# Attention on one Trainium2 chip: reciprocal of the softmax sums read from PSUM, and AV matmuls three chunks behind QK

## The chip, the cores and the metric

The kernel runs on all 8 cores of one Trainium2 chip. Each core computes two of the 16 sequences, with no exchange between cores. The time is device microseconds of the slowest core.

## What is computed

The input x has 16 sequences of 2048 tokens and 1024 features, all float32. One layer with attention (16 heads of 64) and a feed-forward part with a router follows, each with a layer norm in front and one behind:

```python
q = (x @ Wq + bq)                      # 16 heads of 64
k = ((x @ Wk + bk) @ Wl + bl)
v = ((x @ Wv + bv) @ Wl + bl)
attn = jax.nn.softmax(jnp.einsum('bhqd,bhkd->bhqk', q, k) * scale, axis=-1)
out = jnp.einsum('bhqk,bhkd->bhqd', attn, v)
attn_out = out @ Wo + bo
...
x = x + _layernorm(attn_out_of(_layernorm(x)))
x = x + _layernorm(ffn_of(_layernorm(x)))
```

The change lies in the softmax and the product with v alone.

## The kernel before

The program runs five phases with a barrier between them: A0 (norm and projections of the first sequence), B0 (its attention), A1, B1, and C (residual, norms and feed-forward of both sequences). There is no scheduler. Every phase appends small functions to a list for each engine (Q["T"] for PE, Q["V"] for DVE, Q["S"] for ACT, Q["Y"] for the DMA queue of SP), and these lists are each engine's order. inc() raises the engine's semaphore after the last thing appended, and waits are written out by hand. On DVE and ACT, inc() adds a drain (L166), and a wait for it shows in the profile as DVEq L166 or ACTq L166.

Phase B (emit_phase_B, L392) goes over 4 slices of 512 queries (tqc) and in each over 8 pairs of heads (j): 32 pairs in a sequence, 64 in all. For a pair it goes over 16 chunks of 128 keys (tkc):

- emit_qk (L458) multiplies the chunk's keys with the queries of both heads (L467, L471) into one of two PSUM tiles, ps1 or psT (both show as ps or psT, by turns). It waits for the exponential of two chunks before, which frees that tile.
- ACT takes the exponential of the 128x1024 scores (L484) into one of four slots. Two slots are the tile pt_sb, and two lie in xn_tok. It waits for the AV matmuls of four chunks before.
- emit_av (L490) multiplies the exponentials with v for both heads (L499, L502) and adds up over the chunks in av2, 65 rows: 64 of output, and in row 64 the sum of the exponentials, since v has a column of ones. It waits for its exponential, and AV of chunk 0 also for the previous pair's normalisation (attn_done, L493), which reads av2.

The order of the two on PE is set by AVLAG: at step tkc, emit_av(tkc - AVLAG) is appended first and emit_qk(tkc) after it.

After the 16 chunks fden (L519) makes the reciprocals of both heads' sums: 1024 values on one partition. It copies row 64 of av2 (PSUM) to den_sb (SBUF, a part of xn_fm), drains and takes the reciprocal into rden. fdr (L527) spreads them over the partitions by four matmuls with a row of ones (L529, L531), and fnorm (L536) copies these to SBUF (L542) and multiplies (L544, L546) into u_s. In PE's list fdr stands behind the last AV and before the next pair's first QK.

When a slice's 8 pairs are done, its output projection (emit_wo, L413, matmuls L422) is appended to PE in 8 parts among the chunks of the next slice's first pair (j == 0). The last slice of a sequence has it on its own.

Of the kernel before, what the change touches and what calls it, by code (L numbers as in the profile page):

```python
# [31 lines left out]
def build_nc():  # L32
# [33 lines left out]
    with ExitStack() as ctx:  # L66
# [66 lines left out]
        den_sb = fmh[0:1, 0:1024]  # L133
        rden = fmh[0:1, 1024:2048]
# [257 lines left out]
        def emit_phase_B(seq):  # L392
            psTf = psT.bitcast(F32).reshape([128, 1024])
            stb = [ps1[:, 0:1024], psTf[:, 0:1024]]
            av2 = ps2[:, 0:1024]
# [56 lines left out]
            for tqc in range(4):  # L452
                qb = tqc * SLT
                for j in range(8):
# [35 lines left out]
                    def emit_av(tkc):  # L490
                        pp = tkc % 4
                        ed = exp_done[(j, tkc)]
                        wat = attn_done.get(j - 1 if j >= 1 else 7)  # L493
                        def fav(t, j=j, tkc=tkc, pp=pp, ed=ed,
                                avA=avA, avB=avB, wat=wat):
                            t.wait_ge(sS.h, ed)
                            if tkc == 0 and wat is not None:
                                t.wait_ge(sV.h, wat)
                            t.matmul(avA[0:65, :], vt_sb[:, tkc, j, 0:65],  # L499
                                     pslot(pp, 0),  # L500
                                     start=(tkc == 0), stop=(tkc == 15))
                            return t.matmul(avB[0:65, :], vt_sb[:, tkc, j, 65:130],  # L502
                                            pslot(pp, 1),
                                            start=(tkc == 0), stop=(tkc == 15))
                        Q["T"].append(fav)
                        av_done[(j, tkc)] = inc("T", sT)

                    AVLAG = 2
                    for tkc in range(16 + AVLAG):
                        if tkc >= AVLAG:  # L510
                            emit_av(tkc - AVLAG)
                        if tkc < 16:
# [5 lines left out]

                    def fden(v, av2=av2, ad=av_done[(j, 15)]):  # L519
                        v.wait_ge(sT.h, ad)  # L520
                        v.tensor_copy(den_sb[0:1, :], av2[64:65, :])  # L521
                        v.drain()
                        return v.reciprocal(rden[0:1, :], den_sb[0:1, :])  # L523
                    Q["V"].append(fden)
                    den_done = inc("V", sV)
                    drp = drb[par]
# [468 lines left out]
        for ph in phase_list:  # L995
# [21 lines left out]
            elif ph[0] == "B":  # L1017
                seq = int(ph[1])
                load_w("wo", wo_sb)
                barrier()  # L1020
                emit_phase_B(seq)
                barrier()
                if KDBG and seq == 0:
                    qO.n += 16
                    Q["Y"].append(lambda y: y.dma_start(out=ddbg_a, in_=u_s[:]
                                                        ).then_inc(qO.h, 16))
                    qO.n += 16
                    Q["Y"].append(lambda y: y.dma_start(out=ddbg_z0, in_=dzs[0]
                                                        ).then_inc(qO.h, 16))
                    barrier()  # L1030
# [112 lines left out]
```

## Time and profile before

| | us |
|---|---|
| median of 2 runs | 4354.77 (4320.6 and 4388.95) |
| the profiled execution | 4305.65 |
| its span on the slowest core, core 7 | 4304.1 |
| spans of all cores | 4286.0 to 4304.1 |
| PE busy | 2291.9 (53%) |
| DVE busy | 1551.6 (36%) |
| ACT busy | 1310.7 (30%) |

The profile is of one execution. Its span runs from the first to the last instruction of a core. Busy is time in instructions of an engine, PE being TensorE, DVE VectorE and ACT ScalarE. Idle time of an engine is put down to what released it. The granted clock (PEclk) is TensorE's, as a share of full speed: 1.00 is 2.4 GHz and 0.50 is 1.2 GHz.

### The profile page before, as it was taken

How to read it: one execution, taken by the hardware profiler on the slowest of the kernel's cores; microseconds unless marked ns; L12 is line 12 of the kernel's file. 1: busy time of each engine (PE TensorE's matmuls, PEld its weight loads, DVE VectorE, ACT ScalarE, POOL GpSimd, SP SyncE). 2: the span in 40 equal slices, each digit the busy share in tenths (PEclk: the TensorE clock that was granted, in tenths of full speed). 3: DMA queues.
4: the chain of work that ended last, by engine and by line, in shares of the span. 5: the costliest groups of instructions: out<-in, count | busy, mean ns of one | idle time of the engine just before them, and what ended most of it. 6: DMA issues, size and time to landing. Idle time of an engine off the chain costs nothing.

```text
span 4304.1 us, 33363 instructions; the slowest of 8 cores (4286.0 to 4304.1 us)
## 1 busy us (share of the span) xinstructions
PE 2291.9 (53%) x9296; PEld 781.1 (18%) x9296; DVE 1551.6 (36%) x2164; ACT 1310.7 (30%) x1117; POOL 10.1 (0%) x16
## 2 busy tenths in 40 slices
PE   3777555656556554777655655656553333223333
PEld 1333111111111111333211111111111112111121
DVE  2444222323223223444222322323223454455545
ACT  0000355555555550000255555555551000000000
POOL 0000000000000000000000000000000000000000
PEclk9888877777777776888877777777776666566666
DMA  6000100000000003000100000000003212222121
GB/s 119 20 20 1 20 1 0 20 0 0 20 0 20 1 0 78 20 20 1 20 0 0 20 0 1 20 0 20 0 0 88 93 54 83 98 98 98 71 86 59
DMA packets 52842, 137.04 MB, mean 32 GB/s; under 512 B 7479, under 2 KB 7614, under 8 KB 52670
## 3 DMA queue, kind: packets, MB, share of 16 engines
q1 hardware_dynamic: 42206, 117.59, 7.6%
q0 software_dynamic: 10464, 17.32, 2.6%
q8 instruction: 88, 1.44, 0.1%
q14 instruction: 84, 0.69, 0.1%
HBM read 101.87 MB, written 50.33 MB: 35 GB/s over the span
## 4 chain that ended last, share of the span: by engine, by line
PE 36%; DVE 27%; ACT 21%; issue 7%; DMA 5%; DVEq 2%; ACTq 1%; SPq 0%; another core or an unknown queue 0%; POOL 0%; POOLq 0%
PE ps L324 14%; ACT xn_tok L484 10%; DVE xn_fm L523 10%; ACT pt_sb L484 9%; PE ps L499 3%; PE ps L422 3%; PE ps L878 3%; PE ps L529 3%; PE ps L502 2%; DVE xn_fm L521 2%; DMA xst<-z_scr 2%; DVEq L166 2%; PE ps L467 2%; PE psT L467 1%; DVE xn_tok L542 1%
## 5 line engine op out<-in xcount | busy, mean ns | idle before, releaser
L521 DVE COPY xn_fm<-ps 1x1024 f32<-1x1024 f32 x64 | 78.0, 1219 | 1361.3 <-PE ps L502 1361.3
L484 ACT ACTIVATE pt_sb<-ps,cst_sb 128x1024 bf16<-128x1024 f32 x256 | 308.9, 1207 | 779.6 <-PE ps L471 748.1
L523 DVE RECIPROCAL xn_fm<-xn_fm 1x1024 f32<-1x1024 f32 x64 | 418.6, 6541 | 5.1
L529 PE MATMUL ps<-xn_fm,ones_sb 1*64 1x512 f32 x128 | 123.8, 1068 | 520.5 <-DVEq L166 520.5
L324 PE MATMUL ps<-xn_fm,arena 128*128 128x512 bf16 x1536 | 356.0, 395 | 26.3 <-DMA blrow_bf<-blrow 15.5
L499 PE MATMUL ps<-pt_sb,vt_sb 128*65 128x512 bf16 x512 | 223.3, 436 | 262.1 <-ACTq L166 176.2
L484 ACT ACTIVATE xn_tok<-ps,cst_sb 128x1024 bf16<-128x1024 f32 x256 | 308.9, 1207 | 123.8 <-PE ps L471 86.9
L484 ACT ACTIVATE xn_tok<-psT,cst_sb 128x1024 bf16<-128x1024 f32 x256 | 308.8, 1206 | 61.0 <-issue 42.0
L484 ACT ACTIVATE pt_sb<-psT,cst_sb 128x1024 bf16<-128x1024 f32 x256 | 308.8, 1206 | 59.7 <-issue 54.8
L499 PE MATMUL ps<-xn_tok,vt_sb 128*65 128x512 bf16 x512 | 212.6, 415 | 203.3 <-ACTq L166 202.5
L467 PE MATMUL ps<-q_sb,k_sb 64*128 64x512 bf16 x512 | 232.2, 453 | 36.5 <-DMA arena<-wo 36.5
L471 PE MATMUL ps<-q_sb,k_sb 64*128 64x512 bf16 x512 | 232.4, 454 | 0.0
L471 PE MATMUL psT<-q_sb,k_sb 64*128 64x512 bf16 x512 | 229.2, 448 | 0.0
L467 PE MATMUL psT<-q_sb,k_sb 64*128 64x512 bf16 x512 | 229.0, 447 | 0.0
L502 PE MATMUL ps<-pt_sb,vt_sb 128*65 128x512 bf16 x512 | 223.8, 437 | 0.0
L502 PE MATMUL ps<-xn_tok,vt_sb 128*65 128x512 bf16 x512 | 210.7, 412 | 0.0
L277 ACT ACTIVATE sti<-stv 128x4 f32<-128x4 f32 x8 | 1.7, 207 | 646.3 <-DVEq L166 646.3
L596 PE MATMUL ps<-identf_sb,xst 128*128 128x128 f32 x256 | 48.5, 362 | 276.4 <-DMA xst<-z_scr 230.6
L324 PEld LDWEIGHTS ps<-xn_fm,arena 128*128 128x128 bf16 x1536 | 153.4, 101 | 225.0 <-issue 61.3
L735 PE MATMUL psT<-identb_sb,u_s 128*128 128x128 bf16 x256 | 32.4, 305 | 263.9 <-DVEq L166 263.9
L346 DVE TENSOR_SCALAR u_s<-ps,bcols_sb 128x512 bf16<-128x512 f32 x128 | 96.1, 751 | 174.3 <-PE ps L324 174.3
L298 PE MATMUL psT<-identb_sb,xn_tok 128*128 128x128 bf16 x256 | 32.4, 306 | 226.0 <-DVEq L166 226.0
(142 smaller groups left out, 2685.7 us busy)
## 6 DMA issues: line engine op xcount, KB each, us to landing
xst<-x SPq DMA_DIRECT2D x32, 512.0 KB, 7.0
z_scr<-xst SPq DMA_DIRECT2D x64, 256.0 KB, 3.4
xst<-z_scr SPq DMA_DIRECT2D x64, 256.0 KB, 5.3
k_sb<-x SPq DMA_DIRECT2D x32, 512.0 KB, 7.8
x_scr<-q_sb SPq DMA_DIRECT2D x32, 512.0 KB, 2.6
k_sb<-x_scr SPq DMA_DIRECT2D x32, 512.0 KB, 5.1
out<-q_sb SPq DMA_DIRECT2D x32, 512.0 KB, 2.8
arena<-wq POOLq DMA_DIRECT2D x2, 2048.0 KB, 23.1
```

What stands on the lines that cost most here:

```text
L324: r = t.matmul(pa, lhs_get(ki), rhs_get(ki), start=(ki == 0), stop=(ki == n_k - 1 and rider is None))
L346: return v.tensor_scalar(dst_fn(mo), pa, bcols[:, bias0 + mo:bias0 + mo + 1], None, ALU.add)
L422: r = t.matmul(pa, wo_sb[:, ki, mo * 128:(mo + 1) * 128], u_s[:, ki, :], start=(ki == 0), stop=(ki == 7))
L467: t.matmul(stb[pk][:, 0:512], k_sb[0:64, j, tkc * 128:(tkc + 1) * 128], q_sb[0:64, j, qb:qb + SLT], start=True, stop=True, tile_position=( ...
L471: return t.matmul(stb[pk][:, 512:1024], k_sb[64:128, j, tkc * 128:(tkc + 1) * 128], q_sb[64:128, j, qb:qb + SLT], start=True, stop=True, t ...
L484: return sc.activation(pwide(pp), stb[pk][:, 0:1024], AF.Exp, bias=cst[:, 1:2], scale=cst[:, 0:1])
L499: t.matmul(avA[0:65, :], vt_sb[:, tkc, j, 0:65], pslot(pp, 0), start=(tkc == 0), stop=(tkc == 15))
L502: return t.matmul(avB[0:65, :], vt_sb[:, tkc, j, 65:130], pslot(pp, 1), start=(tkc == 0), stop=(tkc == 15))
L521: v.tensor_copy(den_sb[0:1, :], av2[64:65, :])
L523: return v.reciprocal(rden[0:1, :], den_sb[0:1, :])
L529: t.matmul(drp[0:64, :], ones_r[0:1, 0:64], rden[0:1, 0:512], start=True, stop=True, tile_position=(0, 0))
L878: t.matmul(pa, bw_sb[:, ki, mo * 128:(mo + 1) * 128], xn_fm[:, ki, :], start=(ki == 0), stop=False)
```

## The change

Two things are changed, both in phase B. AVLAG goes from 2 to 3, so that each AV is appended one chunk later. And fden no longer copies the sums to SBUF: the reciprocal reads row 64 of av2 in PSUM itself. The copy and the drain behind it are gone. The exponentials' slots, the PSUM tiles and all waits are as before. The lines behind the change stand two lines higher in the changed kernel (L529 is L527 there).

```diff
-                    AVLAG = 2
+                    AVLAG = 3
                     for tkc in range(16 + AVLAG):
                         if tkc >= AVLAG:
                             emit_av(tkc - AVLAG)
...
                     def fden(v, av2=av2, ad=av_done[(j, 15)]):
                         v.wait_ge(sT.h, ad)
-                        v.tensor_copy(den_sb[0:1, :], av2[64:65, :])
-                        v.drain()
-                        return v.reciprocal(rden[0:1, :], den_sb[0:1, :])
+                        return v.reciprocal(rden[0:1, :], av2[64:65, :])
```

PE at the start of the second pair of the first sequence, before. L467 and L471 are QK (into ps1 for even chunks, psT for odd ones), and L499 and L502 are AV:

```order
L467 MATMUL ps1<-q_sb,k_sb 128x512
L471 MATMUL ps1<-q_sb,k_sb 128x512
L467 MATMUL psT<-q_sb,k_sb 128x512
L471 MATMUL psT<-q_sb,k_sb 128x512
L499 MATMUL ps2<-pt_sb,vt_sb 65x512
L502 MATMUL ps2<-pt_sb,vt_sb 65x512
L467 MATMUL ps1<-q_sb,k_sb 128x512
L471 MATMUL ps1<-q_sb,k_sb 128x512
```

The same place in the changed kernel:

```order
L467 MATMUL ps1<-q_sb,k_sb 128x512
L471 MATMUL ps1<-q_sb,k_sb 128x512
L467 MATMUL psT<-q_sb,k_sb 128x512
L471 MATMUL psT<-q_sb,k_sb 128x512
L467 MATMUL ps1<-q_sb,k_sb 128x512
L471 MATMUL ps1<-q_sb,k_sb 128x512
L499 MATMUL ps2<-pt_sb,vt_sb 65x512
L502 MATMUL ps2<-pt_sb,vt_sb 65x512
```

QK of chunk 2 now stands ahead of AV of chunk 0. From there on AV and QK alternate as before, and the pair ends with three AVs in a row instead of two.

PE at the start of a pair that carries the output projection (the first pair of the second slice), before. L422 is one part of the projection, 8 matmuls:

```order
L471 MATMUL psT<-q_sb,k_sb 128x512
L422 MATMUL ps2<-u_s,arena1 128x512 x8
L499 MATMUL ps2<-pt_sb,vt_sb 65x512
L502 MATMUL ps2<-pt_sb,vt_sb 65x512
L467 MATMUL ps1<-q_sb,k_sb 128x512
L471 MATMUL ps1<-q_sb,k_sb 128x512
```

And in the changed kernel:

```order
L471 MATMUL psT<-q_sb,k_sb 128x512
L422 MATMUL ps2<-u_s,arena1 128x512 x8
L467 MATMUL ps1<-q_sb,k_sb 128x512
L471 MATMUL ps1<-q_sb,k_sb 128x512
L499 MATMUL ps2<-pt_sb,vt_sb 65x512
L502 MATMUL ps2<-pt_sb,vt_sb 65x512
```

The projection's part keeps its place behind QK of chunk 1, and QK of chunk 2 and AV of chunk 0 change places behind it.

DVE in one pair, before:

```order
L521 COPY xn_fm<-ps 1x1024
L523 RECIPROCAL xn_fm<-xn_fm 1x1024
L542 COPY xn_tok<-ps 128x512
L544 SCALAR_TENSOR_TENSOR u_s<-ps,xn_tok 64x512
L546 SCALAR_TENSOR_TENSOR u_s<-ps,xn_tok 64x512
```

And in the changed kernel:

```order
L521 RECIPROCAL xn_fm<-ps 1x1024
L540 COPY xn_tok<-ps 128x512
L542 SCALAR_TENSOR_TENSOR u_s<-ps,xn_tok 64x512
L544 SCALAR_TENSOR_TENSOR u_s<-ps,xn_tok 64x512
```

One instruction fewer in each pair, and the source of the reciprocal is now ps.

## Rows read from the trace of the kernel before

**Rows 1.** Windows of phases B0 and B1: us, busy by engine (instructions), PEclk, DMA share, GB/s

```profile
480.00:1636.00 1156.00, 652.94 (x2389) 157.77 (x2390) 333.48 (x186) 619.02 (x513) 0.00 (x0) 0.77 0.02 6
2110.00:3256.00 1146.00, 645.87 (x2373) 155.89 (x2374) 332.17 (x184) 619.03 (x513) 0.00 (x0) 0.78 0.02 6
```

**Rows 2.** Timeline of PE and DVE from one pair to the next: start, duration, [idle before]

```profile
1005.63 0.38 PE L502 MATMUL ps<-xn_tok,vt_sb 128*65 128x512 bf16 x1
1006.11 1.22 DVE L521 COPY xn_fm<-ps 1x1024 f32<-1x1024 f32 x1 [23.00 <-PE ps L502]
1007.41 6.54 DVE L523 RECIPROCAL xn_fm<-xn_fm 1x1024 f32<-1x1024 f32 x1
1014.12 1.08 PE L529 MATMUL ps<-xn_fm,ones_sb 1*64 1x512 f32 x1 [8.12 <-DVEq L166]
...
1016.02 0.60 PE L467 MATMUL ps<-q_sb,k_sb 64*128 64x512 bf16 x1
...
1017.73 0.68 DVE L546 SCALAR_TENSOR_TENSOR u_s<-ps,xn_tok 64x512 bf16<-64x512 f32 x1
...
1018.59 0.60 PE L499 MATMUL ps<-pt_sb,vt_sb 128*65 128x512 bf16 x1 [1.53 <-DVEq L166]
...
1019.56 0.60 PE L467 MATMUL ps<-q_sb,k_sb 64*128 64x512 bf16 x1
...
1021.09 0.60 PE L467 MATMUL psT<-q_sb,k_sb 64*128 64x512 bf16 x1
...
1022.66 0.60 PE L467 MATMUL ps<-q_sb,k_sb 64*128 64x512 bf16 x1
```

**Rows 3.** Timeline of ACT at the same place, exponentials 0 to 4

```profile
1016.79 1.21 ACT L484 ACTIVATE pt_sb<-ps,cst_sb 128x1024 bf16<-128x1024 f32 x1 [11.54 <-PE ps L471]
1018.21 1.21 ACT L484 ACTIVATE pt_sb<-psT,cst_sb 128x1024 bf16<-128x1024 f32 x1 [0.21 <-issue]
1020.32 1.21 ACT L484 ACTIVATE xn_tok<-ps,cst_sb 128x1024 bf16<-128x1024 f32 x1 [0.91 <-PE ps L471]
1021.86 1.21 ACT L484 ACTIVATE xn_tok<-psT,cst_sb 128x1024 bf16<-128x1024 f32 x1 [0.33 <-PE psT L471]
1023.43 1.21 ACT L484 ACTIVATE pt_sb<-ps,cst_sb 128x1024 bf16<-128x1024 f32 x1 [0.37 <-PE ps L471]
```

**Rows 4.** Groups of DVE instructions by line and shape: busy, mean ns, idle before

```profile
L523 DVE RECIPROCAL xn_fm<-xn_fm 1x1024 f32<-1x1024 f32 x64 | 418.6, 6541 | 5.1
...
L521 DVE COPY xn_fm<-ps 1x1024 f32<-1x1024 f32 x64 | 78.0, 1219 | 1361.3 <-PE ps L502 1361.3
...
L252 DVE TENSOR_SCALAR_CACHE_REDUCE pt_sb<-xst 128x1024 f32<-128x1024 f32 x32 | 39.0, 1220 | 46.4 <-DMA xst<-x 39.3 <-issue 7.0
...
L287 DVE TENSOR_SCALAR xn_tok<-xst,stm,sti 128x1024 bf16<-128x1024 f32 x32 | 26.0, 813 | 13.3 <-ACTq L166 6.7 <-issue 6.6
...
L272 DVE RECIPROCAL stv<-stv 128x4 f32<-128x4 f32 x8 | 1.4, 178 | 0.6
```

**Rows 5.** Waits of PE over the span: us in total, times, longest

```profile
PE ps L499 <- DVEq L166: 85.4, 56, 1.5
```

**Rows 6.** Windows (columns as rows 1): in a reciprocal; from a pair's first exponential on

```profile
1010.50:1014.00 3.50, 0.00 (x0) 0.00 (x0) 3.45 (x1) 0.00 (x0) 0.00 (x0) 0.50 0.00 0
1093.66:1101.80 8.14, 6.61 (x19) 1.33 (x18) 1.53 (x3) 6.03 (x5) 0.00 (x0) 0.50 0.00 0
```

**Rows 7.** Waits of ACT over seven pairs of the first sequence, 1093.2 to 1339.5

```profile
ACT pt_sb L484 <- PE ps L471: 83.1, 12, 12.0
...
ACT xn_tok L484 <- PE ps L471: 6.4, 7, 0.9
ACT xn_tok L484 <- PE psT L471: 2.3, 7, 0.3
ACT pt_sb L484 <- PE psT L471: 0.6, 2, 0.3
```

**Rows 8.** Waits of ACT over seven pairs of the second sequence, 2430 to 2677.1

```profile
ACT xn_tok L484 <- PE ps L471: 5.5, 7, 0.9
```

**Rows 9.** Window (columns as rows 1) in a pair that carries the output projection

```profile
1058.00:1082.00 24.00, 24.00 (x113) 8.79 (x112) 5.08 (x7) 16.89 (x14) 0.00 (x0) 1.00 0.00 1
```

## The prediction
> **What bounds the kernel now.** I read the windows by stage first: the two attention stages take 1156 and 1146 us of the 4304.1 us span, and in neither is any engine busy for much over half of it (PE 653, ACT 619, DVE 333 us in the first) [rows 1]. The change touches only them. So the question is which wait ends last in each stretch of one head pair, of which there are 64 (2 sequences, 4 query slices, 8 pairs).
>
> The timeline of one pair's boundary answers it [rows 2]. The last AV matmul (L502) starts at 1005.63, DVE copies the denominators (L521, 1.22 us), computes 1024 reciprocals on one partition (L523, 6.54 us), PE spreads them by matmul (L529, from 1014.12), and only behind that, in PE's order, stand the next pair's QK matmuls (1016.02). ACT sits idle 11.54 us before its first exponential [rows 3]. Everything in that boundary is serial: no other engine works beside it, so a microsecond saved there is a microsecond of the program. Inside a pair, once it runs, the exponentials follow each other with gaps of 0.21 us, one in 1.42 us (1016.79, 1018.21 in [rows 3]): ACT is the bound there and PE waits for it. Between the two lies a short start-up in which ACT waits for PE again: idle 0.91, 0.33 and 0.37 us before exponentials 2, 3 and 4 [rows 3].
>
> **The copy taken out (64 times).** From the start of the copy to the start of the reciprocal is 1007.41 - 1006.11 = 1.30 us [rows 2], copy, drain and issue together. The reciprocal now starts where the copy did, behind the same wait. 64 x 1.30 = 83.2 us, all of it on the path. What I can't read is whether the reciprocal takes 6.54 us when its source is PSUM: no row has that. Two bounds: a copy of 1024 f32 from PSUM takes 1219 ns and a one-element-per-cycle pass over 1024 f32 from SBUF (L252) takes 1220, so the source costs nothing; against that L287, 1024 f32 from SBUF, takes 813, so a source in PSUM could cost up to 0.41 us [rows 4]. Below nothing is excluded, since nothing there makes reading PSUM the quicker. The reciprocal spends (6541 - 178) / 1020 = 6.24 ns on an element (L523 against L272, 4 elements) where the copy spends 1219 / 1024 = 1.19, so its own arithmetic and not its reading should set its pace [rows 4]. I take 0; the other end takes 64 x 0.41 = 26 us back.
>
> The Trainium skill prices this ("VectorE: DVE Perf Modes", the section on the TRN2 errata): a PSUM source has 62 cycles more of fixed cost than one in SBUF, some 65 ns, which by it would be an estimated 4 us less gain in all. The pair L521 and L252 shows no such difference, 1219 against 1220 ns [rows 4], so I leave it out.
>
> **AV one chunk later.** With a lag of 2 the PE order after a boundary is QK0, QK1, AV0, QK2, AV1, QK3; with 3 it is QK0, QK1, QK2, AV0, QK3, AV1. No work is added. What changes is what stands behind AV0. AV0 writes the banks that the previous pair's normalisation still reads, so it waits for L546 to end at 1018.41, and starts at 1018.59 [rows 2]. The waits of PE have this 56 times, 85.4 us, 1.53 each [rows 5]. QK2 stands behind it and begins at 1019.56, though its own condition (exponential 0 done, its bank free) held at 1016.79 + 1.21 = 1018.00. Its result is what ACT waits 0.91 us for.
>
> Now the new start, with this pair's own durations. A released matmul starts 0.18 us after its releaser (1018.41 to 1018.59), and an exponential 0.76 us after its QK (1019.56 to 1020.32) [rows 2, 3]. QK2 starts at 1018.18, exponential 2 could start at 1018.94, and ACT is not free before 1019.63: no stall. Then PE, whose matmuls show 0.60 us here, needs 1.57 us for AV and QK of a chunk (1021.09 to 1022.66 [rows 2]), against ACT's 1.42. QK2 takes 0.53 and AV0 0.97, so QK3 starts at 1019.68 and QK4, 5, 6, 7 at 1021.25, 1022.82, 1024.39, 1025.96; plus 0.76 these release exponentials 3 to 7 at 1020.44, 1022.01, 1023.58, 1025.15 and 1026.72. ACT's slots, 1.42 apart from 1016.79, are at 1021.05, 1022.47, 1023.89, 1025.31 and 1026.73. PE is ahead each time, with the lead just used up at exponential 7, 9.9 us after the first. By then the granted clock is back: of the pairs I looked at, the latest has it at 0.50 until 8.14 us after its first exponential [rows 6]. So the whole start-up stall goes.
>
> Its size, from the waits of ACT over seven pairs [rows 7]: before exponential 2, 6.4 us over 7 waits, less the 7 x 0.21 that stay, 4.9; before exponential 3, 2.3 - 1.5 = 0.8; before 5, 0.6 - 0.4 = 0.2; before 4 (five of the twelve waits in the 83.1 us, at 0.37 each) 5 x 0.16 = 0.8. That is 6.7 us in seven pairs, 0.96 each. In a stretch of the second sequence the first term is 5.5 - 1.5 = 4.0 [rows 8] and a pair gets 0.82. Going through all 56 I find 0.8 to 1.1 with means near 0.93 and 0.81, so 28 x 0.93 + 28 x 0.81 = 49 us; the ends are 0 and 56 x 1.1 = 62.
>
> The other 8 pairs start a query slice. Two begin a sequence and gain half a microsecond each, 1 us. Six carry the output projection of the slice before (L422) between their chunks, and there PE is the bound: busy 24.00 of 24 us [rows 9]. The same matmuls in another order take the same time, so they gain nothing from the lag. The end of a pair doesn't change either: AV15 still goes when exponential 15 is done, with AV13 and AV14 finished before it. Exponential t needs the slot of AV(t-4), which is still issued before QK(t); buffers are enough.
>
> **Sum.** 83 + 49 + 1 = 133 us off the profiled execution of 4305.65, thus 4173. That execution lies 1.1% below the median of the runs, 4354.77, which is the middle of just two (4320.6 and 4388.95). Of the three executions 4320.6 is the middle one; there 133 us off give 4188. I say 4190, 3.0% under that run. A measurement of this kernel can tell about 2%, some 86 us.
>
> **Rivals.**
> The lag brings nothing: PE's slow stretch, 1.57 us a chunk against 1.42, holds ACT back whatever the order, and only the copy pays. Then 4320.6 - 83 = 4237, 1.9% off, no change that can be told. For it speaks that the lead in my table shrinks by 0.15 us a chunk; against it that PE gains the wait of 1.53 us for other work and that the lead lasts until the clock rises.
>
> The clock comes back late or not at all, because a pair's start has other gaps now. Then a pair runs at 1.57 instead of 1.42 for up to 15 chunks, 2.3 us, where the old stall was 0.9: 56 x 1.4 = 78 us eat the copy's 83, and the time is about 4315, no change. Against it: PE would be busier than before in the stretch ahead of the rise, since only the wait before AV0 shrinks. In the stall itself the clock is at 0.50 well before the reciprocal ends [rows 6], so a stall 1.3 us shorter changes nothing there.
>
> The slower one: the reciprocal takes two elements at a time from SBUF and one from PSUM, and doubles. L287 at 813 against the copy's 1219 shows that a source in SBUF is read at more than one element a cycle for some operations [rows 4]. L523 would grow by 1024 x 6.24 = 6.39 us: 64 x 6.39 = 409 lost, 133 won, 276 us slower, 4597. It decides from 133 / 64 = 2.1 us on, a reciprocal of 8.6 us. Against it speaks the 6.24 ns an element, far from any reading rate.
> The Trainium skill has the rule behind this ("VectorE: DVE Perf Modes", "Why PSUM operands drop a tier"): an f32 source in PSUM goes at one element a cycle, where a single-source operation in SBUF can go at two. It lists no reciprocal, and no row here shows a reciprocal on PSUM.
>
> **Chances.** Both parts pay as worked out, or the lag at least in part: 0.81. Lag brings nothing: 0.09. Clock late: 0.04. Reciprocal doubled: 0.05; some other loss 0.01. The range goes from 4140 (62 instead of 49 for the lag, and 0.8% of scatter between runs) to 4270 (only the copy pays, with the same scatter). Faster by over 2%: 0.84, within 2%: 0.10, slower by over 2%: 0.06.
>
> **What would show it.** Right: 64 reciprocals with ps as source at about 6541 ns and no L521 copy; ACT's idle before the first exponential of a pair 11.54 - 1.30 = 10.24 us; 0.21 us before exponentials 2 to 5; PE's 56 waits of 1.53 us before AV0 gone or near 0.6; pairs with L422 shorter by 1.3 us only. Wrong: a reciprocal above 6.6 us; gaps above 0.25 before exponentials 3 to 8; a granted clock that rises later than about 8 us after a pair's first exponential.

## The result, and the profile after

The changed kernel takes 4177.1 us (median of 11 runs) against 4313.58 us (median of 10 runs of the kernel before). The ratio is 0.9714 with a 95% interval of 0.9679 to 0.9749 (the two medians alone would give 0.9684). It is 2.9% faster; the forecast was 3.0%, 4190 us. In some runs the cores of one die show a lower granted clock than the others and take longer, so the ratios leave the slowest runs out, and of e1_copy_out, e3_lag4 and e4_qk2_first the profile is read on cores 1, 2 and 4, each on the die whose clock was higher. The profiled executions went from 4305.65 to 4171.79 us, 133.9 us off, where the sum had said 133.

The groups of DVE's instructions after, which answer to [rows 4] (columns: busy, mean ns of one, idle before):

```profile
L521 DVE RECIPROCAL xn_fm<-ps 1x1024 f32<-1x1024 f32 x64 | 419.3, 6552 | 1313.7 <-PE ps L502 1313.7
```

The copy is gone, and the reciprocal out of PSUM takes 6552 ns where the one out of SBUF took 6541. So the source costs 0.7 us in all, of the 0 to 26 us that the prediction had left open.

ACT's waits over the seven pairs of the first sequence that [rows 7] covered in the kernel before (in us: total, times, longest):

```profile
ACT pt_sb L484 <- PE ps L471: 73.1, 7, 10.7
ACT xn_tok L484 <- issue: 11.9, 56, 0.2
ACT pt_sb L484 <- issue: 10.6, 46, 0.5
ACT pt_sb L484 <- PE ps L502: 0.6, 3, 0.2
```

The 7 waits that are left on PE's QK are the ones before exponential 0. All 56 exponentials with an output in xn_tok (2, 3 and so on) now show no more than their 0.2 us of issue, where [rows 7] had 6.4 and 2.3 us of waits for PE. The wait of 0.2 before three others is that same gap with another releaser named.

The timeline of the same boundary as in [rows 2] and [rows 3], here all engines in one list (weight loads left out):

```profile
975.73 6.55 DVE L521 RECIPROCAL xn_fm<-ps 1x1024 f32<-1x1024 f32 x1 [22.39 <-PE ps L502]
982.46 1.08 PE L527 MATMUL ps<-xn_fm,ones_sb 1*64 1x512 f32 x1 [6.84 <-DVEq L166]
...
984.36 0.60 PE L467 MATMUL ps<-q_sb,k_sb 64*128 64x512 bf16 x1
...
985.12 1.20 ACT L484 ACTIVATE pt_sb<-ps,cst_sb 128x1024 bf16<-128x1024 f32 x1 [10.70 <-PE ps L471]
...
986.49 0.58 PE L467 MATMUL ps<-q_sb,k_sb 64*128 64x512 bf16 x1 [1.10 <-ACTq L166]
...
986.53 1.20 ACT L484 ACTIVATE pt_sb<-psT,cst_sb 128x1024 bf16<-128x1024 f32 x1 [0.21 <-issue]
987.03 0.64 PE L499 MATMUL ps<-pt_sb,vt_sb 128*65 128x512 bf16 x1
...
987.95 1.20 ACT L484 ACTIVATE xn_tok<-ps,cst_sb 128x1024 bf16<-128x1024 f32 x1 [0.21 <-issue]
988.03 0.60 PE L467 MATMUL psT<-q_sb,k_sb 64*128 64x512 bf16 x1
...
989.37 1.20 ACT L484 ACTIVATE xn_tok<-psT,cst_sb 128x1024 bf16<-128x1024 f32 x1 [0.21 <-issue]
```

Read it against the hand-made schedule of the prediction. QK2 was to start 1.39 us after exponential 0, and starts at 986.49 - 985.12 = 1.37. QK3 was to start at 2.89 and does at 2.91. PE's wait of 1.53 us before AV0 has become one of 1.10 before QK2, for exponential 0. Exponentials 1, 2 and 3 follow at 1.41, 1.42 and 1.42 us. AV0 starts at 987.03, when the normalisation before it is done, and over the whole span no wait of AV0 for DVE is left among PE's longest; the one behind the reciprocal is, at every pair (total, times, longest):

```profile
PE ps L527 <- DVEq L166: 437.4, 64, 6.8
```

Read over all pairs from ACT's timeline (in us, from start to start of the exponentials):

| | before | after |
|---|---|---|
| exponential 0 to 15, the 56 normal pairs, sum | 1245.9 | 1196.0 |
| the same, the 2 pairs that begin a sequence, mean | 21.93 | 21.23 |
| the same, the 6 pairs with the output projection, mean | 28.96 | 28.59 |
| exponential 15 to the next pair's 0, 62 times, sum | 793.6 | 718.5 |
| the same, shortest | 12.74 | 11.46 |
| first to last exponential, both sequences | 2257.1 | 2128.5 |

The last row is 128.6 us less. Behind the last exponential of each sequence stands one more reciprocal without its copy, 2 x 1.3 us: 131 of the 134 us lie in the stretches that the change touches.

### The profile page after: what moved, and what is told of

It is laid out like the page before. It is cut to its first block, busy times and chain, and to the rows that moved or that the text cites. A ratio compares the mean times of both kernels' runs of the same rounds, so it can differ in the third digit from the quotient of the medians.

```text
span 4170.3 us, 33235 instructions; the slowest of 8 cores (4155.6 to 4170.3 us)
## 1 busy us (share of the span) xinstructions
PE 2311.7 (55%) x9296; PEld 797.6 (19%) x9296; DVE 1474.4 (35%) x2100; ACT 1307.3 (31%) x1117; POOL 10.1 (0%) x16
## 4 chain that ended last, share of the span: by engine, by line
PE 34%; ACT 25%; DVE 24%; issue 7%; DMA 4%; DVEq 1%; ACTq 1%; SPq 1%; another core or an unknown queue 0%; POOL 0%; POOLq 0%
PE ps L324 14%; ACT xn_tok L484 12%; ACT pt_sb L484 12%; DVE xn_fm L521 10%; PE ps L422 3%; PE ps L876 3%; PE ps L527 3%; PE ps L499 2%; PE ps L467 2%; PE ps L502 2%; DMA xst<-z_scr 2%; DVE k_sb L908 1%; DVE k_sb L604 1%; DVE pt_sb L676 1%; DVE pt_sb L256 1%
## 5 line engine op out<-in xcount | busy, mean ns | idle before, releaser
L521 DVE RECIPROCAL xn_fm<-ps 1x1024 f32<-1x1024 f32 x64 | 419.3, 6552 | 1313.7 <-PE ps L502 1313.7
L527 PE MATMUL ps<-xn_fm,ones_sb 1*64 1x512 f32 x128 | 123.8, 1068 | 437.4 <-DVEq L166 437.4
L467 PE MATMUL ps<-q_sb,k_sb 64*128 64x512 bf16 x512 | 232.8, 455 | 223.7 <-ACTq L166 187.7
L467 PE MATMUL psT<-q_sb,k_sb 64*128 64x512 bf16 x512 | 229.4, 448 | 131.9 <-ACTq L166 130.4
L499 PE MATMUL ps<-xn_tok,vt_sb 128*65 128x512 bf16 x512 | 221.0, 432 | 75.2 <-ACTq L166 75.2
L471 PE MATMUL ps<-q_sb,k_sb 64*128 64x512 bf16 x512 | 237.9, 465 | 0.0
L499 PE MATMUL ps<-pt_sb,vt_sb 128*65 128x512 bf16 x512 | 234.4, 458 | 0.0
L471 PE MATMUL psT<-q_sb,k_sb 64*128 64x512 bf16 x512 | 233.6, 456 | 0.0
L502 PE MATMUL ps<-pt_sb,vt_sb 128*65 128x512 bf16 x512 | 224.3, 438 | 0.0
L502 PE MATMUL ps<-xn_tok,vt_sb 128*65 128x512 bf16 x512 | 211.1, 412 | 0.0
L467 PEld LDWEIGHTS ps<-q_sb,k_sb 64*128 64x128 bf16 x512 | 48.9, 96 | 577.3 <-issue 577.3
```

The costliest lines, as they stand in the source:

```text
L467: t.matmul(stb[pk][:, 0:512], k_sb[0:64, j, tkc * 128:(tkc + 1) * 128], q_sb[0:64, j, qb:qb + SLT], start=True, stop=True, tile_position=( ...
L471: return t.matmul(stb[pk][:, 512:1024], k_sb[64:128, j, tkc * 128:(tkc + 1) * 128], q_sb[64:128, j, qb:qb + SLT], start=True, stop=True, t ...
L499: t.matmul(avA[0:65, :], vt_sb[:, tkc, j, 0:65], pslot(pp, 0), start=(tkc == 0), stop=(tkc == 15))
L502: return t.matmul(avB[0:65, :], vt_sb[:, tkc, j, 65:130], pslot(pp, 1), start=(tkc == 0), stop=(tkc == 15))
L521: return v.reciprocal(rden[0:1, :], av2[64:65, :])
L527: t.matmul(drp[0:64, :], ones_r[0:1, 0:64], rden[0:1, 0:512], start=True, stop=True, tile_position=(0, 0))
```

## The experiments

All ratios are to the kernel before, run on the same chip in the same rounds.

### The first part alone

```diff
-                    AVLAG = 3
+                    AVLAG = 2
```

(to the changed kernel, so the copy is out and the order is the old one.)

> The change without its first part: AVLAG stays 2, and the reciprocal reads PSUM. My theory: the two parts add up and this one is worth 64 x 1.29 us, less up to 5 us where the clock falls before the last AV, so a ratio to before of 0.981 to 0.983 (78 to 82 us off); the waits of 0.91, 0.33 and 0.37 us before exponentials 2, 3 and 4 and PE's 56 waits of 1.53 us before AV0 are as in the kernel before. Rival (the parts depend on each other, the shorter stall is what let the start-up run without a gap): those waits shrink here too and the ratio is near 0.975.

Measured: ratio 0.9851 (0.9781 to 0.9922). The two sequences take 2182.9 us from first to last exponential, 74.2 less than before, and with the two reciprocals at the ends 77 us. Between pairs the shortest is 11.46 us, as in the changed kernel. PE's waits over the span, and ACT's over seven pairs:

```profile
PE ps L499 <- DVEq L166: 85.4, 56, 1.5
```

```profile
ACT xn_tok L484 <- PE ps L471: 6.4, 7, 0.9
ACT xn_tok L484 <- PE psT L471: 2.3, 7, 0.3
```

These are the numbers of [rows 5] and [rows 7], to the tenth. The ratio lies above my range of 0.981 to 0.983, but its interval holds it and leaves out the rival's 0.975, and the waits say the same more sharply. The rival falls: with 1.3 us less in the stall ahead of it, the start-up stall is as long as before.

### The second part alone

```diff
-                    AVLAG = 2
+                    AVLAG = 3
```

(to the kernel before, so the copy stays.)

> The change without its second part: AVLAG is 3, the copy stays. My theory: 49 to 53 us off, a ratio of 0.988; exponentials 0 to 15 of a normal pair in 21.24 us as in the changed kernel, and 12.75 us from the last exponential of a pair to the first of the next. Rival (the start-up stall goes only where the stall before it is short): gaps above 1.42 us between exponentials 2 to 5 remain and the ratio is over 0.993.

Measured: ratio 0.9892 (0.9832 to 0.9952), and 2200.8 us from first to last exponential of both sequences, 56.3 less than before (49 to 53 expected; the last section says where the rest comes from). ACT's waits over seven pairs:

```profile
ACT pt_sb L484 <- PE ps L471: 81.3, 7, 12.0
ACT xn_tok L484 <- issue: 11.9, 56, 0.2
ACT pt_sb L484 <- issue: 9.8, 42, 0.5
ACT pt_sb L484 <- PE ps L502: 1.5, 7, 0.2
```

Only the seven waits before exponential 0 are left, and they are the long ones of the kernel before (12.0 at most, 10.7 without the copy). A normal pair has its 16 exponentials in 21.25 us, or in 21.53 where one of the gaps is 0.28 us longer for no wait that the profile shows. That is the gap before exponential 1 or 8 in 24 of the 56, here as in the other kernels, the kernel before included. The time between pairs is 12.75 us, as expected, and 13.21 behind the six pairs with the projection. The interval of the ratio alone reaches past the rival's 0.993; the waits refute it. So this part is worth 56 us, and the two parts, 74.2 and 56.3, add up to 130.5 where both together gave 128.6.

### One chunk more

```diff
-                    AVLAG = 3
+                    AVLAG = 4
```

> The changed kernel with AVLAG 4: QK3 too stands ahead of AV0. My theory: no exponential of a normal pair waits for PE any more at lag 3, so nothing is left to gain; same time as the changed kernel within 0.3%, ratio to before 0.970 to 0.973. Rival (PE's order still limits in the pairs with the output projection or after the clock rises late): up to 10 us less. Second rival (exponential 4 waits for the slot of AV0, which now stands behind QK3): gaps before exponential 4 of 0.3 us or more, up to 20 us slower than the changed kernel.

Measured: ratio 0.9659 (0.9627 to 0.9691), median 4170.6, 0.16% under the changed kernel's 4177.1 (the intervals of the two ratios overlap). Normal pairs take 21.25 us again (21.53 in 24 of the 56), exponential 4 comes on time, which refutes the second rival, and first to last exponential is 2123.5 us in both sequences, 5.0 less. In the six pairs with the projection 3.2 us are gained (28.06 us against 28.59), and 2.6 of them are lost again behind these pairs (12.36 against 11.92). The other 56 boundaries take 11.46 or 11.47 us each, and that is the larger part: in the changed kernel 13 of them are longer, those in which the clock falls ahead of the last AV (see "The copy" below). So the first rival's "up to 10 us less" has the size, but not the place. There was nothing left to win in the start-up, as the lead computed in the prediction said. The ratio lies just under the range that I had given.

### QK2 ahead of AV0, and then a lag of 2 again

The order at the start of a pair is QK0, QK1, QK2, AV0, AV1, QK3, AV2, QK4 (to the changed kernel):

```diff
-                    AVLAG = 3
+                    AVLAG = 2
                     for tkc in range(16 + AVLAG):
-                        if tkc >= AVLAG:
+                        if tkc > AVLAG:
+                            if tkc == AVLAG + 1:
+                                emit_av(0)
                             emit_av(tkc - AVLAG)
```

> The changed kernel, but only QK2 is put ahead of AV0; then AV0 and AV1 run in a row before QK3 and the lag is 2 again. It tells why a lag of 3 takes the whole start-up stall away. My theory: both QK2's place ahead of AV0's wait and the lead that the late AV gives in the slow-clock stretch are needed. Two AVs in a row at 0.97 us each put QK3 at 3.86 us after exponential 0, so exponential 3 starts 0.37 us late and 4 and 5 some 0.15 us late each: of the 0.93 us stall 0.6 remains, and the kernel is some 25 to 35 us slower than the changed one (ratio to before 0.977 to 0.980). Rival: only passing AV0's wait counts; then exponentials 3 to 5 come on time and the time is that of the changed kernel (0.971).

Measured: ratio 0.9778 (0.9722 to 0.9834), which barely leaves out the rival's 0.971; the waits decide. First to last exponential takes 2147.4 us in both sequences, 18.9 more than in the changed kernel, where 25 to 35 had been expected. The timeline at a pair's start:

```profile
992.71 1.20 ACT L484 ACTIVATE pt_sb<-ps,cst_sb 128x1024 bf16<-128x1024 f32 x1 [10.26 <-PE ps L471]
...
994.62 0.64 PE L499 MATMUL ps<-pt_sb,vt_sb 128*65 128x512 bf16 x1
...
995.50 0.61 PE L499 MATMUL ps<-pt_sb,vt_sb 128*65 128x512 bf16 x1
...
996.47 0.61 PE L467 MATMUL psT<-q_sb,k_sb 64*128 64x512 bf16 x1
...
997.24 1.20 ACT L484 ACTIVATE xn_tok<-psT,cst_sb 128x1024 bf16<-128x1024 f32 x1 [0.49 <-PE psT L471]
```

QK3 starts 3.76 us after exponential 0 (3.86 had been expected), and exponential 3 waits 0.49 us, 0.28 more than the usual gap, as it does in all 56 normal pairs. So the rival falls. A normal pair keeps 0.36 us of its stall (1216.1 us in all 56 against 1196.0), where I had expected 0.6: exponentials 4 and 5 are late by 0.15 or less, and only in some pairs. So the mechanism holds, and the size was two thirds too large. Of the 0.89 us that a lag of 3 takes away in the mean, going past AV0's wait alone gives 0.53, and having one AV instead of two ahead of QK3 the remaining 0.36. How much of this 0.36 is due to the low clock, at which the AVs run there, no run separates.

### The reciprocal behind the spreading

Nothing in the change touches the 6.55 us reciprocal, which is the larger part of the 11.46 us between pairs. If what stands ahead of QK0 in PE's order is what counts, then it can be moved: the sums are copied and spread first, and each partition takes the reciprocal of 512 of them (to the changed kernel).

```diff
-                        return v.reciprocal(rden[0:1, :], av2[64:65, :])
+                        return v.tensor_copy(rden[0:1, :], av2[64:65, :])
...
-                        v.tensor_copy(dr_sb[:], drp)
+                        v.reciprocal(dr_sb[:], drp)
```

> Built on the changed kernel (lag 3): fden copies the 1024 sums from PSUM to SBUF, the matmuls spread the sums, and fnorm takes the reciprocal of 128x512 from PSUM instead of copying 128x512. The 6.55 us reciprocal on one partition leaves the stretch ahead of the next pair's QK. My theory: the time between pairs is what stands ahead of QK0 in PE's order, so it goes from 11.46 to about 6.1 us; the reciprocal of 512 elements takes 3.35 us (178 + 508 x 6.24 ns) and lets AV0 go 2.7 us later than now, 4.5 us after exponential 0; QK3 stands behind AV0, so exponential 3 is some 1.9 us late. Net 3.1 us a pair, about 195 us in all, ratio to before 0.920 to 0.930, less if the clock now stays up over the shorter stall. Rival: AV0's wait is what counts, and everything slides with it: 2.7 us a pair, 170 us.

Measured: 3957.93 us (median), 3942.25 in the profiled execution, ratio 0.9178 (0.9072 to 0.9284), a little better than my range. The timeline:

```profile
924.43 1.22 DVE L521 COPY xn_fm<-ps 1x1024 f32<-1x1024 f32 x1 [21.42 <-PE ps L502]
925.83 0.61 PE L527 MATMUL ps<-xn_fm,ones_sb 1*64 1x512 f32 x1 [1.50 <-DVEq L166]
...
926.83 0.39 PE L467 MATMUL ps<-q_sb,k_sb 64*128 64x512 bf16 x1
...
927.08 3.36 DVE L540 RECIPROCAL xn_tok<-ps 128x512 f32<-128x512 f32 x1 [1.43 <-PE ps L529]
927.38 1.20 ACT L484 ACTIVATE pt_sb<-ps,cst_sb 128x1024 bf16<-128x1024 f32 x1 [3.81 <-PE ps L471]
...
932.07 0.61 PE L499 MATMUL ps<-pt_sb,vt_sb 128*65 128x512 bf16 x1 [2.71 <-DVEq L166]
...
933.81 1.20 ACT L484 ACTIVATE xn_tok<-psT,cst_sb 128x1024 bf16<-128x1024 f32 x1 [2.39 <-PE psT L471]
```

The reciprocal takes 3.36 us (3.35 expected) and lies beside the exponentials. AV0 goes 4.69 us after exponential 0 (4.5 expected), and QK3 behind it makes exponential 3 wait 2.39 us, 2.18 over the usual gap (1.94 in the mean of the normal pairs, 1.9 expected). The start-up stall is back, because AV0's wait is long again. The gain over the changed kernel, 229.5 us between the profiled executions (219 between the medians), is more than the 195 of the sum. Most of the difference is the clock, which stays up in a part of the boundaries: there L527 takes 0.61 us instead of 1.08. In 12 of the 62 boundaries the time between pairs is 5.01 or 5.02 us, its shortest; in 17 it is 6.13, with L527 at 1.08, close to the 6.1 expected. The mean is 5.67, and 62 times the 0.43 below 6.1 are 27 us.

### The same with a lag of 4

```diff
-                    AVLAG = 3
+                    AVLAG = 4
```

(to the kernel of e5_spread_first.)

> As e5_spread_first with a lag of 4, so that QK3 stands ahead of AV0 too. My theory: the lag is worth something exactly as far as AV0's wait is long. Here the wait is 2.7 us longer, so chunk 3 ahead of it pays, where it paid nothing in the changed kernel: exponential 3 comes on time, exponential 4 some 0.5 us late, net 4.5 us a pair, about 275 us in all, ratio to before 0.900 to 0.912 and 60 to 90 us faster than e5_spread_first. Rival (a lag beyond 3 is worth nothing, as in e3_lag4): same as e5_spread_first within 0.3%.

Measured: 3838.78 us, ratio 0.8907 (0.8880 to 0.8933). It is 338 us under the changed kernel's median. From e5_spread_first to it the profiled execution goes from 3942.25 to 3838.22 us, 104 less (119 between the medians). The ratio is better than the expected range, and so is the distance to e5_spread_first.

```profile
904.44 1.20 ACT L484 ACTIVATE pt_sb<-psT,cst_sb 128x1024 bf16<-128x1024 f32 x1 [0.21 <-issue]
905.81 0.58 PE L467 MATMUL psT<-q_sb,k_sb 64*128 64x512 bf16 x1 [0.81 <-ACTq L166]
...
907.27 1.20 ACT L484 ACTIVATE xn_tok<-psT,cst_sb 128x1024 bf16<-128x1024 f32 x1 [0.21 <-issue]
907.71 0.61 PE L499 MATMUL ps<-pt_sb,vt_sb 128*65 128x512 bf16 x1 [1.29 <-DVEq L166]
...
909.44 1.20 ACT L484 ACTIVATE pt_sb<-ps,cst_sb 128x1024 bf16<-128x1024 f32 x1 [0.97 <-PE ps L471]
```

QK3 (905.81) no longer waits for AV0, and exponential 3 comes on time; exponential 4 waits 0.97 us, 0.76 over the gap (0.68 in the mean, 0.5 expected). The same lag of 4 that gave 0.16% on the changed kernel gives 2.6% here. In these kernels a chunk more of lag paid in the start-up where PE still waited for DVE ahead of AV0 (1.53 us in the kernel before, 2.71 in e5_spread_first) and paid nothing there where it didn't (the changed kernel).

The part that I had not priced is the clock. A window over the last 4.5 us of a pair and the boundary behind it in this kernel, and one inside the stall of the changed kernel (columns as in rows 1):

```profile
895.00:903.00 8.00, 5.04 (x22) 1.37 (x22) 1.50 (x2) 3.61 (x3) 0.00 (x0) 0.99 0.00 0
```

```profile
975.80:980.00 4.20, 0.00 (x0) 0.00 (x0) 4.20 (x1) 0.00 (x0) 0.00 (x0) 0.50 0.00 0
```

PE's longest wait in this boundary is 1.50 us instead of 6.84, and the granted clock is still high through the spreading and the first QK. It is so before all 64 spreadings, in each of which the first L527 takes 0.61 us:

```profile
PE ps L527 <- DVEq L166: 96.0, 64, 1.5
```

The time between pairs is 5.10 us in the mean of 62, a microsecond less than the 6.1 that I had worked out with durations at the low clock. That is 62 us, about the whole distance from the expected 275 us to the 333.6 between the profiled executions of the changed kernel and this one.

## Why the prediction was right

**What bounds it.** That a boundary is serial, and that a microsecond saved there is one of the program, held: the shortest went from 12.74 to 11.46 us, and e1_copy_out alone showed it with everything else as before. e5_spread_first then showed from the other side that it is PE's order which makes it serial.

**The copy.** 83.2 us were forecast. Between pairs 75.1 went, and 2.6 at the two ends, 77.7. The missing 5.5 are made of known pieces. The shortest boundary is 1.28 us less instead of 1.30, and half of that difference is the reciprocal's 11 ns; it makes 1.3 us in all. In the six pairs with the projection one AV more stands behind the last QK, so that the time behind the pair is 0.46 us longer than elsewhere (11.92 against 11.46), 2.8 us in all where it was about 1 before; about as much is gained inside these pairs. The prediction had said that the end of a pair doesn't change, and for these six it does. The rest, some 2.5 us, is the clock at the last AV. In 13 of the 56 normal pairs it falls within 1.7 us of the start of exponential 15, and so before or at the last AV, and just these 13 have boundaries 0.2 to 0.45 us longer than the shortest; before there were 6 of this kind. In the boundary shown above the last AV's second matmul has 0.63 us where the one in [rows 2] has 0.38:

```profile
974.99 0.63 PE L502 MATMUL ps<-xn_tok,vt_sb 128*65 128x512 bf16 x1
```

I had taken the clock into account only inside the stall and at its rise.

**The lag.** 49 us were forecast for the 56 normal pairs, and 1245.9 - 1196.0 = 49.9 came. The whole stall went, in each of them. (In single pairs it had been 0.56 to 1.12 us, a wider spread than the 0.8 to 1.1 of the prediction; the two means, 0.94 and 0.81, are as it has them.) The two first pairs gained 0.7 us each instead of 0.5. The six with the projection gained 0.37 us each inside and gave 0.28 back behind, so next to nothing, as forecast; what else they vary by is the clock (below).

**The base.** The sum was right to 1 us on the profiled execution, 133.9 against 133. A part of this closeness is luck: the copy brought 5.5 us less than its term, and what made up for it are 0.9 us in the normal pairs, 0.4 in the two first ones, 2.2 inside the six with the projection, and 2.7 us outside the stretches that the change touches, for which the sum had no term. The forecast of 4190 missed by 13: 7 of these are its base, 4320.6 where the median of ten runs is 4313.58, and 2 are its rounding from 4188.

**The rivals.** That the lag brings nothing is refuted by e2_lag3_only; the two-element reciprocal by 6552 ns; the late clock by its rise, which comes 4.5 to 7.9 us after the first exponential in the 56 normal pairs (5.0 to 8.2 before), and by those pairs, in which no exponential from 1 to 15 waits for PE. (Gaps above 0.25 us, which the prediction had named as a sign of being wrong, do stand before exponential 8 in 12 of them, but they are the ones of 0.28 us over the usual that the kernel before has too.) On the reciprocal the Trainium skill ("VectorE: DVE Perf Modes", "Why PSUM operands drop a tier") says that an f32 operand in PSUM holds an operation to one element a cycle. The trace doesn't contradict this, but the reciprocal never used more: with 1024 elements on one partition and 512 on 128, both from PSUM, (6552 - 3357) / 512 is 6.24 ns an element, the same as out of SBUF. The 3357 ns are the mean of the 64 in e6_spread_lag4. The Trainium skill ("VectorE: DVE Perf Modes", the section on the TRN2 errata) gives PSUM 62 cycles more of fixed cost, an estimated 65 ns; the measured difference is 11 ns, and the measurement decides.

## What to carry to other kernels

In a loop with an accumulator that the previous round still reads, put independent work ahead of its first writer, as much as fits into the writer's wait: the profile gives the wait, and the lag to try follows from it. More than that gained nothing in the start-up here (e3_lag4). Then take every instruction that the next round doesn't need out of what stands ahead of it in the in-order queue; that a step is on the path is often only its place. Where a change shortens a stall, durations taken from the low-clock stretch behind it can be too long: here L527 went from 1.08 to 0.61 us when PE's wait ahead of it went from 6.84 to 1.50.

## What the runs showed of the hardware that I had not expected

A reciprocal costs 6.24 ns an element of the free dimension, on one partition as on 128, and out of PSUM as out of SBUF (6552, 6541 and 3357 ns). A DVE copy of 1024 out of PSUM costs 1.19. So 1024 sums on one partition took 6.55 us, and the same sums spread over 128 partitions, each 64 times over, took 3.36.

The pairs with the projection, in which PE is the bound, are as long as the clock makes them. In the kernel before, the clock rises between 4.56 and 7.12 us after the pair's first exponential, and exponential 0 to 15 takes 28.18 to 29.35 us, in this order: some 0.46 us longer for each microsecond that it rises later. In e2_lag3_only it rises at 4.8 to 5.1 us in all six, and they take 27.87 to 28.00. At that rate the earlier rise is some 4 of the 7 us that this kernel gained beyond the 49. What decides when the clock rises no run here shows, and none tried to steer it.
